# Wide attention with another order of its small steps, the first split of maxima ahead of two loads, and the last stores no longer waited for in their own stage

## The chip, the cores and the metric

The kernel runs on one core of one Trainium2 chip. Its five engines each follow their own list of instructions: TensorE (PE, with PEld for its weight loads), VectorE (DVE), ScalarE (ACT), GpSimd (POOL) and SyncE (SP), which here only issues transfers. They meet at semaphores. The metric is the device time of one execution in microseconds (us). Shorter is better.

## The reference

The model adds four blocks to `x` (8 batches, 512 rows, 256 columns); the context `ctx` has 1601 rows a batch.

```
x = x + tanh(g_xattn[0]) * attention_16_heads(layernorm(x), ctx, ctx)      # L0, bias bo on its output
x = x + tanh(g_ffn[0])   * one_of_4_experts(layernorm(x))
x = x + tanh(g_xattn[1]) * attention_1_head(layernorm(x), ctx, ctx)        # L1, rank-16 terms in Q, K, V
x = x + tanh(g_ffn[1])   * product_key_memory(batchnorm over rows, x)      # top 8 of 64 x 64 keys, 8 heads
```

In the wide (one-head) attention the products of weights are folded beforehand, so that per batch it is: `g = A xn^T`, scores `s = ctx g` (1601 x 512), softmax over the 1601 keys, `u = ctx^T p`, output `u^T C` divided by the sum of the probabilities and added to `x`.

## The kernel before

Five stages follow each other: `project`, `attend_heads`, `experts`, `attend_wide`, `memory`. Each is one block of code per engine. At the end of a block the engines meet before the next block starts. There is no scheduler: each engine does what the code lists, in that order, and an instruction that waits holds up all behind it.

**Wide attention (`attend_wide`).** One iteration `b` of 8 has these steps.

- PE: 13 score tiles of 128 keys (L1354, two matmuls each, which the trace shows as four rows), with small jobs hung behind certain tiles: the output product of batch `b-2` (`out_product`, L1394) behind tile `OUT_AT`, the transposes of the next normalised rows (L1322) behind `NORMS_AT`, the product with A (L1340) behind `MIX_AT`, the transposes of the finished rows of batch `b-3` (L1330) behind `LAST_AT`. Then `u` of batch `b-1`, two passes of 13 tiles (L1387). Within the first pass it transposes the running maxima (`turn_top`, L1365) and spreads them over the keys (`spread_rows`, L1372); within the second it sums the probabilities (`sums`, L1379). Score tile `kt` waits until ACT has emptied the buffer of tile `kt-4`.
- ACT: copies each score tile to `aw_sT` (L1492), then 13 exponentials (L1502), then a square root for the norm of batch `b+2` (L1464), one for the norm of the finished batch `b-2`, and then the copy of `u` to `aw_uT` (L1468, called by `copy`), for which `out_product` waits.
- DVE: running maxima (L1565), peaks (L1570, L1571), 13 subtractions `shift` (L1577), `invert` (the factor of one over the sum, L1583 and L1584), then `norms(b+2)` (L1525 and the lines of the helper `norm_tiles`: L91, L95, L97, L99, L101) and `last_norms(b-2)` with the same helper. A square root on ACT waits for L97 of its norm.
- POOL: gathers rows, then adds the 13 tiles of probabilities to `aw_total` (L1638). The first addition of batch `b` waits for `sums(b-1)`, which reads the same buffer.
- SP: stores the finished rows and their transposes (`last_out`, L1295, L1298), and at the stage's end waits for all these stores (L1314).

**Start of `attend_heads`.** SP loads the operands of four groups of heads, about 2.5 MB each (L422, L424, L431, L433, L457), the bias `bo` (L478), and with `rows_out` (L464) the three bfloat16 parts of the maxima of group 0. The first scores of unit 0 (L576) wait for these three, and those of unit 1 for its own three. The parts come from POOL's `split` (L773 to L776). POOL's list there is `spread`, `spread`, `split(0)`, `add_bias`, `split(1)`; `add_bias` (L789, L793) waits for `bo`.

**Start of `memory`.** POOL loads the transposed rows of tile 0 (L1769) and normalises them (L1778) for the first scores of PE (L1803); SP loads the two key tables of 4 MB (L1734) after the first two row tiles have landed. PE's first L1830 waits for the second table.

Of the kernel before, what the change touches and what calls it, by code (L numbers as in the profile page):

```python
# [22 lines left out]
P = 128  # L23
B, S, D = 8, 512, 256
KEYS = 1601
KC = D // P
# [5 lines left out]
G = H // HG  # L32
# [27 lines left out]
def gate(eng, sem):  # L60


    eng.sem_inc(sem, 1)
# [282 lines left out]
def attend_heads(nc, sem, t):  # L346
# [38 lines left out]
    with Stage(nc, "at") as st:  # L385
# [57 lines left out]
        with nc.Block() as block:  # L443
            @block.sync
            def _(sp):
# [30 lines left out]
                for g in range(G - 1):  # L476
                    load(0, g, False)
                sp.dma_start(bo[:, :], t["bo_in"]).then_inc(bo_in, 16)  # L478
                rows_out(0, 0)
# [746 lines left out]
def attend_wide(nc, sem, t):  # L1226
# [9 lines left out]
    NORMS_AT, OUT_AT, MIX_AT, LAST_AT = 4, 1, 7, 9  # L1236
    ROWS_AT, TOTAL_AT = (4, 9), 6
# [5 lines left out]
    with Stage(nc, "aw") as st:  # L1243
# [19 lines left out]
        l_turned, l_out, l_counted, l_stored = (sem(f"aw_last_{n}") for n in ("turned", "out", "counted", "stored"))  # L1263
# [5 lines left out]
        def turned_max(b):  # L1269

            return 2 + 3 * (b - 1) + 1 if b else 1
# [5 lines left out]
        def sums_mm(b):  # L1277

            return 2 + 3 * (b + 1) if b < B - 1 else 2 + 3 * (B - 1) + 1
# [3 lines left out]
        with nc.Block() as block:  # L1283
            @block.sync
            def _(sp):
# [28 lines left out]
                sp.wait_ge(l_stored, 16 * (1 + KC) * B + 1)  # L1314

            @block.tensor
            def _(pe):
# [57 lines left out]
                def sums(b):  # L1375

                    pe.wait_ge(summed, (b + 1) * (KT - 1))
                    for q in range(QT):
                        ins = nc.tensor.matmul(ps_p[:, 1, 0, q:q + 1], total[:, q * P:q * P + P], ones[:, 0:1], start=True, stop=True)  # L1379
                    ins.then_inc(peaks_mm, 1)  # L1380
# [26 lines left out]
                for b in range(B):  # L1407
# [18 lines left out]
                    for kt in range(KT):  # L1426
                        u_tile(b - 1, 0, kt)
                        if kt == ROWS_AT[0]:
                            turn_top(b)
                        elif kt == ROWS_AT[1]:  # L1430
                            spread_rows(b)
                    for kt in range(KT):
                        ins = u_tile(b - 1, 1, kt)
                        if kt == TOTAL_AT:
                            sums(b - 1)
# [24 lines left out]
            def _(act):  # L1460
# [22 lines left out]
                for b in range(B):  # L1483
# [19 lines left out]
                    if b + 2 < B:  # L1503
                        root(nth["next", b + 2])
                    if b >= 2:
                        root(nth["last", b - 2])
                    if b:
                        copy(uT[:, :, :], u_at[b - 1], u_mm, b, uT_out)
# [9 lines left out]
            def _(dve):  # L1518
# [72 lines left out]
                for b in range(B):  # L1591
# [4 lines left out]
                    if b >= 3:  # L1596
                        last_stats(b - 3)
                    find_peaks(b)
# [3 lines left out]
                    if b:  # L1602
                        invert(b - 1)
# [52 lines left out]
def memory(nc, sem, t, out):  # L1656
# [18 lines left out]
    with Stage(nc, "mt") as st:  # L1675
# [5 lines left out]
        xl, xb = st.sb("xl", [P, 2, KC, P]), st.sb("xb", [P, 2, KC, P])  # L1681
# [18 lines left out]
        mk, scale, offset = t["mk"], st.sb("scale", [P, KC]), st.sb("offset", [P, KC])  # L1700
        gamma, beta = t["gamma"], t["beta"]
        bmv, bve, bsd = st.sb("bmv", [P, KC, 2]), st.sb("bve", [P, KC]), st.sb("bsd", [P, KC])
# [23 lines left out]
        with nc.Block() as block:  # L1726
            @block.sync
            def _(sp):
                sp.dma_start(iota_f, t["m_iota_in"]).then_inc(iota_in, 16)
# [31 lines left out]
            def _(pool):  # L1761
                def token_rows(i, off):

                    n, s = 2 * i + off, off % 2
                    if off > 1:

                        pool.wait_ge(d_mm, (n - 1) * ND)
                        gate(pool, t["pool_gate"])
                    pool.dma_start(xl[:, s, :, :], t["xT_dram"][n]).then_inc(xl_in[s], 16)  # L1769
# [115 lines left out]
            def _(act):  # L1885
# [35 lines left out]
                def first():  # L1921
                    act.wait_ge(b_var, 1)
                    nc.scalar.activation(bsd[:, :], bve[:, :], ACT.Sqrt).then_inc(b_sd, 1)
                    for c in range(2):
                        scores_out(0, 0, c)
# [172 lines left out]
def build(nc, ins, out, debug=None):  # L2098

    with ExitStack() as ctx:  # L2100
        def sem(name):
# [36 lines left out]
            "gates_opened": sem("gates_opened"), "release_x": x_life.close, "bstats": bstats,  # L2138
# [103 lines left out]
```

## Time and profile before

| | us |
|---|---|
| median of 3 runs (3486.71 to 3490.65) | 3489.04 |
| the profiled execution, whole | 3490.57 |
| its span in the trace | 3488.9 |
| project (PE's last wait before heads ends) | 0 to 231.6 |
| heads, first scores of unit 0 | from 293.66 |
| wide attention, first transposes to last statistics | 1784.1 to 2295.3 |
| memory | 2298.8 to the end |

Over the span PE is busy 95%, DVE 72%, ACT 46% and POOL 13%. In a row of the timeline the first number is the start, the second the stretch that the merged instructions cover, and the brackets at its end hold the idle time just before it on that engine and who ended it. All times are us from the start of the span. A "releaser" is who signalled last.

### The profile page before, as it was taken

Reading aid. Unit: us, or ns where it says so; the run is one execution under the profiler, and the core shown is the slowest. Engines: PE = TensorE matmul, PEld = TensorE weight load, DVE = VectorE, ACT = ScalarE, POOL = GpSimd, SP = SyncE. Lnnn points to the kernel's source line nnn. Section 1 sums busy time; section 2 is a strip of 40 time slices with the busy share of each in tenths; the row PEclk is TensorE's granted clock in tenths of the full one; section 3 lists DMA queues with packets and bytes.
Section 4 is the critical chain, followed back from the end, with each engine's and each line's share of the span. In section 5 each row is a group of like instructions: output and inputs, shape, how many; then the busy total and the mean of one; then the engine's idle time right before and its main releaser. Section 6 shows DMA issues by size and latency. Waiting matters only on the chain. (4 is left out here: it accounts for less than half of the span.)

```text
span 3488.9 us, 61035 instructions
## 1 busy us (share of the span) xinstructions
PE 3307.3 (95%) x21500; PEld 1962.3 (56%) x21500; DVE 2506.5 (72%) x5513; ACT 1602.7 (46%) x2882; POOL 452.8 (13%) x538
## 2 busy tenths in 40 slices
PE   9988999999999999779979989969999999999999
PEld 5652222222222222568844444538889888898988
DVE  5557898889898986520035565568888888888885
ACT  5535888888888888212223323312222222222221
POOL 0022111111111100110014241300000000000000
PEclk9987999999999999879989999979999999999999
DMA  7687676757575650421111221130000000000000
GB/s 275 247 232 96 99 105 100 105 100 105 100 106 99 94 72 15 171 92 49 38 63 50 75 81 62 43 129 10 11 12 11 12 9 11 12 11 12 9 12 8
DMA packets 148231, 256.70 MB, mean 74 GB/s; under 512 B 23848, under 2 KB 99472, under 8 KB 147536
## 3 DMA queue, kind: packets, MB, share of 16 engines
q1 hardware_dynamic: 132752, 218.29, 29.4%
q0 software_dynamic: 10288, 31.21, 2.7%
q10 hardware_dynamic: 5008, 5.00, 0.5%
q8 instruction: 86, 1.41, 0.2%
q14 instruction: 97, 0.79, 0.1%
HBM read 170.38 MB, written 83.64 MB: 73 GB/s over the span
## 5 line engine op out<-in xcount | busy, mean ns | idle before, releaser
L724 DVE TENSOR_REDUCE at_pmax<-at_psm 128x2 f32<-128x1024 f32 (+1 forms) x832 | 945.0, 1179 | 127.7 <-PE at_psm L552 123.0
L661 ACT ACTIVATE ring<-at_pss 128x512 f32<-128x512 f32 (+1 forms) x1664 | 895.1, 595 | 194.0 <-PE at_pss L576 190.9
L576 PE MATMUL at_pss<-at_qs,at_ks 99*128 99x512 bf16 (+1 forms) x1664 | 512.0, 386 | 14.7 <-ACT ring L661 7.2
L1830 PE MATMUL mt_psd<-mt_xl,mt_key_in 128*128 128x128 f32 x4096 | 491.8, 279 | 0.2 <-DMA mt_key_out<-m_out 0.2
L1830 PEld LDWEIGHTS mt_psd<-mt_xl,mt_key_in 128*128 128x128 f32 x4096 | 470.3, 193 | 1.6 <-DMA mt_key_out<-m_out 0.3
L1856 PE MATMUL mt_psu<-mt_key_out,mt_g 128*128 128x256 f32 x2048 | 447.4, 379 | 1.3 <-DVE mt_g L2066 1.3
L584 PE MATMUL at_pso<-ring,at_vw 128*32 128x512 f32 (+1 forms) x3328 | 444.0, 605 | 0.0
L1856 PEld LDWEIGHTS mt_psu<-mt_key_out,mt_g 128*128 128x128 f32 x2048 | 386.7, 190 | 52.6 <-DVE mt_g L2066 1.4
L576 PEld LDWEIGHTS at_pss<-at_qs,at_ks 99*128 99x128 bf16 (+1 forms) x1664 | 116.5, 98 | 489.7 <-ACT ring L661 428.0
L1918 ACT ACTIVATE mt_g<-mt_psd 128x512 f32<-128x512 f32 x256 | 152.9, 598 | 349.7 <-PE mt_psd L1830 349.4
L550 PE MATMUL at_psm<-at_ks,at_qs 64*128 64x512 bf16 (+1 forms) x1024 | 272.1, 344 | 10.2 <-DVE at_pmax L724 8.9
L552 PE MATMUL at_psm<-at_kh,at_qh 64*128 64x512 bf16 (+1 forms) x1024 | 272.4, 344 | 0.0
L550 PEld LDWEIGHTS at_psm<-at_ks,at_qs 64*128 64x128 bf16 x1024 | 78.5, 94 | 228.6 <-issue 152.0
L2066 DVE TENSOR_TENSOR mt_g<-mt_psc,mt_g 128x512 f32<-128x512 f32 x256 | 164.0, 683 | 56.8 <-PE mt_psc L1845 56.2
L1894 ACT ACTIVATE mt_sims<-mt_psx 128x512 f32<-128x512 f32 x64 | 38.3, 598 | 349.8 <-PE mt_psx L1803 349.8
L1354 PE MATMUL aw_pss<-aw_gT,wide_ctxT 128*128 128x512 f32 (+1 forms) x416 | 186.9, 599 | 5.0 <-DVE aw_sT L1577 2.8
L1845 PEld LDWEIGHTS mt_psc<-mt_hot_w,mt_hot_m 128*128 128x128 f16 x4096 | 136.8, 98 | 36.2 <-issue 34.8
L1196 ACT ACTIVATE ex_hid<-ex_psh,ex_b 128x256 f32<-128x256 f32 x136 | 62.5, 474 | 205.9 <-PE ex_psh L1161 205.8
L1565 DVE TENSOR_TENSOR aw_top<-aw_top,aw_sT 128x512 f32<-128x512 f32 (+1 forms) x88 | 64.5, 732 | 127.7 <-ACT aw_sT L1492 127.1
L584 PEld LDWEIGHTS at_pso<-ring,at_vw 128*32 128x32 f32 (+1 forms) x3328 | 65.8, 108 | 152.4 <-ACT ring L661 130.1
L2036 DVE TENSOR_TENSOR mt_hot_m<-mt_iota_m,mt_picksT 128x2048 f16<-128x2048 f16 x128 | 150.2, 1213 | 0.0
L1769 POOL DMA_DIRECT2D mt_xl<-xT_dram x32 | 18.6, 580 | 1012.4 <-PE mt_psd L1830 976.7
(232 smaller groups left out, 4193.1 us busy)
## 6 DMA issues: line engine op xcount, KB each, us to landing
at_ks<-k_dram SPq DMA_DIRECT2D x192, 200.1 KB, 6.4
k_dram<-pj_kp SPq DMA_DIRECT2D x24, 800.5 KB, 5.4
xs_dram<-at_qf POOLq DMA_DIRECT2D x68, 256.0 KB, 3.1
v_dram<-pj_v SPq DMA_DIRECT2D x8, 1664.0 KB, 6.6
at_vd<-v_dram SPq DMA_DIRECT2D x32, 416.0 KB, 10.1
wide_ctxT<-ctxT SPq DMA_DIRECT2D x8, 1601.0 KB, 7.2
at_kh<-k_dram SPq DMA_DIRECT2D x124, 100.1 KB, 5.4
at_qs<-q_dram SPq DMA_DIRECT2D x192, 64.0 KB, 6.8
```

Of the source, the lines that this page charges most:

```text
L550: nc.tensor.matmul(ps_m[:, n % MBANKS, 0, to:to + w], qs[0:MAX_ROWS, g, 2 * p, q * P:q * P + P], ks[0:MAX_ROWS, g, 2 * p, a:a + w], start= ...
L552: ins = nc.tensor.matmul(ps_m[:, n % MBANKS, 1, to:to + w], qh[MAX_ROWS:2 * MAX_ROWS, g, p, q * P:q * P + P], kh[MAX_ROWS:2 * MAX_ROWS, g, ...
L576: nc.tensor.matmul(ps_s[0:r, score_slot(u, n), :], ks[:, g, j, kt * P:kt * P + r], qs[:, g, j, :], start=True, stop=True).then_inc(s_mm, 1)
L584: nc.tensor.matmul(ps_o[j * 32:(j + 1) * 32, :], vw[0:r, g % 2, kt * HG + j, :], pr[0:r, (NST * g + n) % PRING, :], start=kt == 0, stop=kt ...
L661: nc.scalar.activation(pr[0:r, (NST * g + n) % PRING, :], ps_s[0:r, score_slot(u, n), :], ACT.Exp, scale=SCALE).then_inc(expd, 1)
L724: nc.vector.tensor_reduce(heads, found, AX.X, ALU.max).then_inc(m_red, 1)
L1354: ins = nc.tensor.matmul(ps_s[0:r, slot(b, kt), :], ctxT[:, b % 2, k, kt * P:kt * P + r], gT[:, b % 2, k, :], start=k == 0, stop=k == KC - 1)
L1830: ins = nc.tensor.matmul(ps_d[:, j % 2, y * P:y * P + P], key_in[:, k, j * YB + y, :], xl[:, s, k, :], start=k == 0, stop=k == KC - 1)
L1856: ins = nc.tensor.matmul(ps_u[:, 0:D], g[:, off % 2, y, :], key_out[:, y, :], start=y == 0, stop=y == YH - 1)
L1918: nc.scalar.activation(g[:, off % 2, j * YB:(j + 1) * YB, :], ps_d[:, j % 2, :].rearrange("p (y n) -> p y n", n=P), ACT.Gelu).then_inc(g_o ...
L2036: return nc.vector.tensor_tensor(dst.rearrange("p n (m r) -> p n m r", r=RUN), iota[:, 0:cols].rearrange("p (m r) -> p m r", r=RUN).unsque ...
L2066: nc.vector.tensor_tensor(gv, ps_c[:, tb % CRING, h, :].rearrange("p (n u y) -> p y u n", u=2, y=YH), gv, ALU.mult).then_inc(w_out, 1)
```

## The change

In `attend_heads` SP issues the maxima of group 0 behind two loads of groups instead of three; the third load and the bias come behind them. In `attend_wide` the small jobs of PE move to later tiles, `sums(b-1)` moves from the second pass of `u` to the first, ahead of `turn_top`, ACT copies `aw_uT` ahead of the second square root, and DVE calls `invert` ahead of `find_peaks`. SP no longer waits for the last stores at the end of the stage; instead those in `memory` who read the stored rows, or whose buffers may lie where the stored rows lay, wait for the same semaphore, and POOL's first two loads only for the stores of the first batch. `sums` gets two waits more, for ACT's copies of transposes out of the bank that it writes.

```diff
@@ attend_heads, SP
-                for g in range(G - 1):
+                for g in range(2):
                     load(0, g, False)
+                rows_out(0, 0)
+                load(0, 2, False)
                 sp.dma_start(bo[:, :], t["bo_in"]).then_inc(bo_in, 16)
-                rows_out(0, 0)
                 load(0, G - 1, False)
                 rows_out(0, 1)
@@ attend_wide
-    NORMS_AT, OUT_AT, MIX_AT, LAST_AT = 4, 1, 7, 9
-    ROWS_AT, TOTAL_AT = (4, 9), 6
+    NORMS_AT, OUT_AT, MIX_AT, LAST_AT = 6, 2, 9, 11
+    ROWS_AT = (4, 9)
...
-                sp.wait_ge(l_stored, 16 * (1 + KC) * B + 1)
@@ PE
                 def sums(b):
                     pe.wait_ge(summed, (b + 1) * (KT - 1))
+                    pe.wait_ge(xnT_out, min(b + 3, B))
+                    if b >= 2:
+                        pe.wait_ge(l_out, b - 1)
...
                         if kt == ROWS_AT[0]:
+                            sums(b - 1)
                             turn_top(b)
...
                         ins = u_tile(b - 1, 1, kt)
-                        if kt == TOTAL_AT:
-                            sums(b - 1)
@@ ACT
                         root(nth["next", b + 2])
+                    if b:
+                        copy(uT[:, :, :], u_at[b - 1], u_mm, b, uT_out)
                     if b >= 2:
                         root(nth["last", b - 2])
-                    if b:
-                        copy(uT[:, :, :], u_at[b - 1], u_mm, b, uT_out)
@@ DVE
+                    if b:
+                        invert(b - 1)
                     find_peaks(b)
                     dve.wait_ge(peaks_mm, max_rows(b))
                     for kt in range(KT):
                         shift(b, kt)
-                    if b:
-                        invert(b - 1)
@@ memory, SP
+                sp.wait_ge(t["wide_stored"], PER_BATCH * B + 1)
                 sp.dma_start(iota_f, t["m_iota_in"]).then_inc(iota_in, 16)
@@ memory, POOL
+                    pool.wait_ge(t["wide_stored"], PER_BATCH * (B if off > 1 else 1) + 1)
                     pool.dma_start(xl[:, s, :, :], t["xT_dram"][n]).then_inc(xl_in[s], 16)
@@ memory, ACT, behind the square root
+                    act.wait_ge(t["wide_stored"], PER_BATCH * B + 1)
```

ACT, wide attention, from the exponentials of one batch to the score tiles of the next; `aw_sd` is a square root, `aw_uT` the copy of `u`. Before:

```order
L1502 ACTIVATE aw_sT<-aw_sT 65x512
L1464 ACT_TABLE_LOAD
L1464 ACTIVATE aw_sd<-aw_ve 128x4 x2
L1468 ACTIVATE aw_uT<-aw_psw 128x1024
L1492 ACTIVATE aw_sT<-aw_pss 128x512 x6
```

And now:

```order
L1505 ACTIVATE aw_sT<-aw_sT 65x512
L1467 ACT_TABLE_LOAD
L1467 ACTIVATE aw_sd<-aw_ve 128x4
L1471 ACTIVATE aw_uT<-aw_psw 128x1024
L1467 ACTIVATE aw_sd<-aw_ve 128x4
L1495 ACTIVATE aw_sT<-aw_pss 128x512 x8
```

The copy of `u` stands between the two roots; the score tiles still stand behind both.

PE, wide attention, from the first pass of `u` to the next batch's norms; `aw_psp<-aw_ones,aw_total` are the sums, `cmat` marks the output product. Before:

```order
L1387 MATMUL aw_psw<-aw_sT,aw_ctx 128x512 x5
L1365 MATMUL aw_psp<-ident_sb,aw_top 128x128 x4
L1387 MATMUL aw_psw<-aw_sT,aw_ctx 128x512 x5
L1372 MATMUL aw_pss<-aw_rows,aw_ones 128x512
L1387 MATMUL aw_psw<-aw_sT,aw_ctx 128x512 x10
L1379 MATMUL aw_psp<-aw_ones,aw_total 128x1 x4
L1387 MATMUL aw_psw<-aw_sT,aw_ctx 128x512 x6
L1354 MATMUL aw_pss<-aw_gT,wide_ctxT 128x512 x4
L1394 MATMUL aw_psw<-cmat,aw_uT 128x256 x8
L1354 MATMUL aw_pss<-aw_gT,wide_ctxT 128x512 x6
L1322 MATMUL aw_psp<-ident_sb,aw_xn 128x128 x8
```

And now:

```order
L1391 MATMUL aw_psw<-aw_sT,aw_ctx 128x512 x5
L1383 MATMUL aw_psp<-aw_ones,aw_total 128x1 x4
L1366 MATMUL aw_psp<-ident_sb,aw_top 128x128 x4
L1391 MATMUL aw_psw<-aw_sT,aw_ctx 128x512 x5
L1373 MATMUL aw_pss<-aw_rows,aw_ones 128x512
L1391 MATMUL aw_psw<-aw_sT,aw_ctx 128x512 x16
L1355 MATMUL aw_pss<-aw_gT,wide_ctxT 128x512 x6
L1398 MATMUL aw_psw<-cmat,aw_uT 128x256 x8
L1355 MATMUL aw_pss<-aw_gT,wide_ctxT 128x512 x8
L1323 MATMUL aw_psp<-ident_sb,aw_xn 128x128 x8
```

The sums stand 16 matmuls of `u` earlier, the output product one tile later, the transposes two tiles later. The matmuls are the same.

SP, start of `attend_heads`, from the end of the third group's load (before) and of the second's (now) on; `at_mpart` are the parts of the maxima. Before:

```order
L457 DMA at_vd<-v_dram 128x832
L478 DMA at_bo<-bo 128x256
L464 DMA at_qs<-at_mpart 1x16x128 x3
L422 DMA at_ks<-k_dram 16x4x1601
L424 DMA at_qs<-q_dram 16x4x512
```

And now:

```order
L457 DMA at_vd<-v_dram 128x832
L464 DMA at_qs<-at_mpart 1x16x128 x3
L422 DMA at_ks<-k_dram 16x4x1601
...
L457 DMA at_vd<-v_dram 128x832
L480 DMA at_bo<-bo 128x256
L422 DMA at_ks<-k_dram 16x4x1601
```

The parts stand ahead of the third group's 21 transfers, and the bias with these behind the parts.

## Rows read from the trace of the kernel before

**Rows 1.** Windows (start:end, length, busy time of each engine, clock, DMA), wide attention.
```profile
1888.10:1942.70 54.60, 54.60 (x151) 26.59 (x150) 31.11 (x49) 21.08 (x32) 21.09 (x17) 1.00 0.21 70
...
2082.00:2086.00 4.00, 4.00 (x11) 3.14 (x10) 3.10 (x4) 0.00 (x0) 3.40 (x4) 0.50 0.05 11
```

**Rows 2.** Waits of PE, 1820 to 2300: in total, times, longest.
```profile
PE aw_psw L1394 <- ACT aw_uT L1468: 25.5, 5, 6.3
```

**Rows 3.** Timeline of PE, wide attention, batches 3, 5 and 7.
```profile
1942.74 3.60 PE L1354 MATMUL aw_pss<-aw_gT,wide_ctxT 128*128 128x512 f32 x8
...
2071.16 3.60 PE L1354 MATMUL aw_pss<-aw_gT,wide_ctxT 128*128 128x512 f32 x8
2081.03 6.34 PE L1394 MATMUL aw_psw<-cmat,aw_uT 128*128 128x256 f32 x16 [6.28 <-ACT aw_uT L1468]
...
2092.36 1.04 PE L1322 MATMUL aw_psp<-ident_sb,aw_xn 128*128 128x128 f32 x8
...
2200.53 3.60 PE L1354 MATMUL aw_pss<-aw_gT,wide_ctxT 128*128 128x512 f32 x8
```

**Rows 4.** Timeline of ACT, turn from batch 4 to 5.
```profile
2071.41 0.20 ACT L1464 ACTIVATE aw_sd<-aw_ve 128x4 f32<-128x4 f32 x1 [4.86 <-DVE aw_ve L97]
2079.86 0.20 ACT L1464 ACTIVATE aw_sd<-aw_ve 128x4 f32<-128x4 f32 x1 [8.24 <-DVE aw_ve L97]
2079.97 1.01 ACT L1468 ACTIVATE aw_uT<-aw_psw 128x1024 f32<-128x1024 f32 x1
```

**Rows 5.** Timeline of DVE, turn from batch 4 to 5.
```profile
2056.72 7.86 DVE L1577 TENSOR_TENSOR aw_sT<-aw_sT,aw_pss 128x512 f32<-128x512 f32 x13 [3.73 <-PE aw_pss L1372]
...
2067.54 1.28 DVE L1525 SCALAR_TENSOR_TENSOR x_rows<-aw_y,opened_sb,x_rows 128x1024 f32<-128x1024 f32 x1
...
2079.01 0.82 DVE L97 TENSOR_SCALAR aw_ve<-aw_mv 128x4 f32<-128x4 f32 x1
```

**Rows 6.** Timeline of POOL, turn from batch 4 to 5.
```profile
2066.21 1.27 POOL L1638 TENSOR_TENSOR aw_total<-aw_sT 128x512 f32<-128x512 f32 x1 [41.72 <-PE aw_psp L1379]
```

**Rows 7.** Timelines of DVE and POOL, batch 0.
```profile
1826.43 7.86 DVE L1577 TENSOR_TENSOR aw_sT<-aw_sT,aw_pss 128x512 f32<-128x512 f32 x13 [1.22 <-PE aw_pss L1372]
1834.21 1.27 DVE L1525 SCALAR_TENSOR_TENSOR x_rows<-aw_y,opened_sb,x_rows 128x1024 f32<-128x1024 f32 x1
...
1828.46 1.27 POOL L1638 TENSOR_TENSOR aw_total<-aw_sT 128x512 f32<-128x512 f32 x1 [35.82 <-ACT aw_sT L1502]
```

**Rows 8.** Timeline of PE, scores of batch 1.
```profile
1843.86 1.85 PE L1322 MATMUL aw_psp<-ident_sb,aw_xn 128*128 128x128 f32 x8 [3.05 <-DVE aw_xn L101]
1845.50 6.28 PE L1354 MATMUL aw_pss<-aw_gT,wide_ctxT 128*128 128x512 f32 x12
```

**Rows 9.** SP's wait and a row of the chain, turn to memory.
```profile
SPq L1283 <- DMA xT_dram<-keys: 2.5, 1, 2.5
...
2299.28 2.52 DMA mt_xl<-xT_dram
```

**Rows 10.** Timeline, start of heads; last row: issue to landing of the maxima's transfers.
```profile
271.86 0.88 POOL L762 COPY at_vw<-at_vd 128x832 f32<-128x832 f32 x1 [14.26 <-DMA at_vd<-v_dram]
...
283.28 1.89 SPq L464 DMA_DIRECT2D at_qs<-at_mpart  x3
...
292.35 0.93 POOL L789 TENSOR_SCALAR at_bo<-at_bo,opened_sb 128x256 f32<-128x256 f32 x1 [9.10 <-DMA at_bo<-bo]
293.37 18.55 POOL L793 TENSOR_TENSOR x_rows<-x_rows,at_bo 128x1024 f32<-128x1024 f32 x8
293.66 1.44 PE L576 MATMUL at_pss<-at_qs,at_ks 99*128 99x512 bf16 x3 [6.74 <-DMA at_qs<-at_mpart]
...
323.69 0.28 POOL L773 CAST at_mpart<-at_mfull 16x128 bf16<-16x128 f32 x1 [11.78 <-ACT at_mfull L677]
...
330.36 0.60 PE L576 MATMUL at_pss<-at_qs,at_ks 99*128 99x512 bf16 x2
...
DMA to landing us min/median/max: 1.7/2.3/8.8
```

More of the change, by code:

```diff
@@ L1262, in attend_wide @@
         u_mm, uT_out, o_mm, o_out = (sem(f"aw_{n}") for n in ("u_mm", "uT_out", "o_mm", "o_out"))
-        l_turned, l_out, l_counted, l_stored = (sem(f"aw_last_{n}") for n in ("turned", "out", "counted", "stored"))
+        l_turned, l_out, l_counted = (sem(f"aw_last_{n}") for n in ("turned", "out", "counted"))
+        l_stored = t["wide_stored"]
         def slot(b, kt):
@@ L1269, in turned_max @@
         def turned_max(b):
-            return 2 + 3 * (b - 1) + 1 if b else 1
+            return 2 + 3 * (b - 1) + 2 if b else 1
         def max_rows(b):
@@ L1277, in sums_mm @@
         def sums_mm(b):
-            return 2 + 3 * (b + 1) if b < B - 1 else 2 + 3 * (B - 1) + 1
+            return 2 + 3 * b + 1
         u_at = [ps_w[:, :, :]] * (B - 1) + [ps_s[:, 0:KC, :]]
@@ L1680, in memory @@
         gate_down = st.sb("gate_down", [P, 1])
-        xl, xb = st.sb("xl", [P, 2, KC, P]), st.sb("xb", [P, 2, KC, P])
         xr = st.sb("xr", [P, 2, D])
@@ L1700, in memory @@
         mk, scale, offset = t["mk"], st.sb("scale", [P, KC]), st.sb("offset", [P, KC])
+        PER_BATCH = 16 * (1 + KC)
         gamma, beta = t["gamma"], t["beta"]
+        xl, xb = st.sb("xl", [P, 2, KC, P]), st.sb("xb", [P, 2, KC, P])
         bmv, bve, bsd = st.sb("bmv", [P, KC, 2]), st.sb("bve", [P, KC]), st.sb("bsd", [P, KC])
@@ L2137, in build @@
             "ident": ident, "ident_in": ins["ident"], "gates": gates, "gates_in": ins["gates"], "opened": opened,
-            "gates_opened": sem("gates_opened"), "release_x": x_life.close, "bstats": bstats,
+            "gates_opened": sem("gates_opened"), "wide_stored": sem("aw_last_stored"), "release_x": x_life.close, "bstats": bstats,
             "x_dram": nc.dram_tensor("x_dram", (NT, P, D), F32, kind="Internal").ap(),
```

## The prediction

> **What bounds the kernel now.** I read the busy shares first: PE is busy for 95% of the span, so a change that adds no matmul can only win where PE stands idle or runs at the lower clock. The list of PE's waits in wide attention names the place: it waited 25.5 us for the copy `aw_uT`, in 5 waits of which the longest is 6.3 [rows 2]. The timeline shows one [rows 3]: after two score tiles of batch 5 (2071.16 to 2074.75) PE idles 6.28 us and takes the output product at 2081.03. That row covers 6.34 us, and the window from 2082 to 2086 shows why it is long: the granted clock is 0.50, which is 1.2 instead of 2.4 GHz [rows 1]. ACT's rows name the cause [rows 4]: the copy runs at 2079.97, right behind a second square root at 2079.86 that had waited 8.24 us for DVE, while `u` had been ready since about 2071.2. A neighbour gives the size of a batch without the wait: from 1888.10 to 1942.70 (batch 2) PE is busy 54.60 of 54.60 us at clock 1.00 [rows 1]. Batches 3 to 6 take (2200.53 - 1942.74) / 4 = 64.45 us each [rows 3].
>
> **Wide attention, batches 3 to 6.** These batches hold the work of batch 2 and one group of eight transposes more, at most 1.04 us [rows 3], so 55.64 us with no wait. The stake is 64.45 - 55.64 = 8.81 us a batch: 6.28 of idle time, the rest lower clock. It is won if `aw_uT` is there when PE wants it, and if nothing else is late. I follow the turn from batch 4 to 5.
>
> PE now does the sums (some 0.8 us) ahead of the transposes of the maxima, so the spread of the maxima and DVE's subtractions move from 2056.72 to 2057.5 [rows 5]. They take 7.86 and end at 2065.4. POOL's first addition waited until 2066.21 for the sums [rows 6]; now only the exponentials hold it. Batch 0 is the pattern, since it has no sums ahead of it [rows 7]: the additions start 2.03 us after the subtractions, here at 2059.6, and beside them the 13 subtractions still take 7.86. `invert` no longer stands behind the subtractions. There it cost DVE the way from 2064.6 to 2067.54 [rows 5], so the norm starts at 2065.4 instead of 2067.54, and the first root, 3.9 us behind that start [rows 4, 5], comes at 2069.3 instead of 2071.41. The next instruction on ACT is now the copy, which waits only for the end of `u`. PE's work up to there is the same, so the copy runs at about 2071.4 to 2072.4. PE wants it after three tiles, at 2071.16 + 3 x 1.72 = 2076.3. Cover: 3.9 us.
>
> What is late next is the second root: the first score tile's copy stands behind it on ACT, and PE's fifth tile waits for that. DVE reached the second L97 at 2079.01, 11.47 us behind the start of the norm [rows 5]; from 2065.4 that is 2076.9, with its 0.82 us 2077.7, and the root and the first copy end by 2078.6. PE reaches its fifth tile at 2076.3 + 3.4 (output product) + 1.7 (fourth tile) = 2081.5. Cover: 2.9 us. So I take the whole stake, 4 x 8.81 = 35.2 us. The bounds are nothing lost, 35.2, and a new stall of the old kind in each batch, which keeps nothing.
>
> A rule of the Trainium skill bears on that cover. First the row: the fused addition at 1834.21 began straight behind the subtractions and took 1.27 with POOL adding beside it [rows 7], no longer than the 1.28 at 2067.54 [rows 5]. In "SBUF — State Buffer", section "Who interferes with whom", the skill says that a DVE instruction with both inputs in SBUF contends with a GpSimd instruction that reads SBUF, and that the one that comes second is blocked for the whole of the other. By that rule the fused addition would have to wait for one addition of 1.27 now that POOL runs from 2059.6; by the row it waits for none. With the wait the cover shrinks from 2.9 to 1.6 us and the sum stays; two such waits and a little more would open the first rival below, and I put 3 of its hundredths there.
>
> **Batch 1.** PE waited 3.05 us for DVE's `aw_xn` before the transposes, which then took 1.85 instead of 1.04, and twelve rows took 6.28 where eight take 3.60, so twelve about 5.3 [rows 3, 8]. The transposes now stand two tiles later, and two tiles are 3.4 us, more than the wait. Gain 3.05 + 0.81 + 0.95 = 4.8 us. Bounds: 3.05 if the clock stays low as long, 4.8 if not. I take 4.8, since the work that fills the gap is matmul work. Batches 2 and 7 had no such wait and keep their time. The later places of the other jobs cost nothing: each keeps its distance to its reader, and the transposes of the finished rows are read by ACT 2.5 us before the sums want the bank.
>
> **Turn to memory.** SP waited 2.5 us for the last stores before the engines could meet [rows 9]. Without it POOL's load of tile 0 moves from 2299.28 up by 2.5. It took 2.52 us and now runs beside those stores, 768 KB. I take 2.2 us; bounds 1.5 and 2.5. DVE's statistics, the two key tables and all behind them move with it, since the tables wait for the two row tiles. ACT and SP wait for the last stores in the new place until about 2298.4, earlier than their next work is due, and POOL's two other waits are met.
>
> **Heads, start.** PE waited 6.74 us for the maxima's parts, to 293.66; they had been issued from 283.28 on but took up to 8.8 instead of the median 2.3 us, behind the load of group 2 [rows 10]. Now only loads 0 and 1 stand ahead, and these had landed at 271.86. The third part is issued at about 284.6 and lands at 286.9, so unit 0 starts at 287.0, 6.7 us earlier. But the bias lands behind load 2, which starts only at 285.2. From 271.86 to 292.35 that pair took 20.5 us when it queued behind others; fresh, I take 19.8, so it lands at 305.0. The bounds are 299.8 (at the 14.6 us in which the next load of the same size passed, until the DMA engines went quiet at 306.9) and 305.7. Then POOL's bias takes 19.6 us (292.35 to 311.92 [rows 10]) to 324.6, and `split(1)` stands behind it on POOL. Before, it began at 323.69 after an idle of 11.78; now it would be wanted at 317.0 and begins at 324.6. From its start to the landing of the last part are 1.7 (281.62 to 283.28 for unit 0) + 1.3 (to the issue of the third) + 2.3 = 5.3 us, so unit 1 can start at 329.9. It started at 330.36 [rows 10] and PE would now be there at 323.7: a stall of 6.2 us, of the size that in wide attention brought the clock to 0.50. There it cost 8.81 - 6.28 = 2.5 us; PE is the busiest engine here too, but its matmuls are less dense: 2.0. So heads give 0.5 and take 2.0: 1.5 us slower. Bounds: 6.7 faster (bias early enough) and 2.5 slower.
>
> **Sum.** -35.2 - 4.8 - 2.2 + 1.5 = -40.7 us. The profiled execution took 3490.57 us, so 3449.9; it stands 1.5 above the median of the runs, from which the same sum gives 3448.3. I predict 3448.5.
>
> **The rivals.**
> - *The second root takes the copy's place.* PE stops at the fifth tile instead. For it: the cover of 2.9 us rests on DVE beside POOL, where a scalar operation takes up to 1.3 us instead of 0.35. Against: even a root as late as the old one (2079.86) lets the fifth tile go by 2080.9. If it stops PE by 2 us with 2 of low clock behind, 4 batches lose 16: 3465.
> - *The whole gain of heads stays.* The bias lands by about 299, so `split(1)` is in time: 8 us less, 3441. For it: the next load passed in 14.6 us. Against: it had been queued while another ran.
> - *Slower.* POOL's additions now lie beside the 13 subtractions in every batch. If each had to wait for an addition, 1.3 us instead of 0.6, they would take 17 and end 9.3 us later; `aw_uT` would come at 2079.9, a stall of 3.6 + 2 in the tails of batches 1 to 6, and 5.5 before `u` of batch 7. The fifth tile would wait 2 more in four of them. That is 6 x 5.6 + 5.5 + 8 = 47 against 40.0 gained: less the 0.7 that the other parts give, 3497, and it decides from 1.13 us a subtraction on. Against it: 7.86 us for 13 beside POOL in batch 0 [rows 7].
> - *The change doesn't do what it says*, with the wait kept by a condition that I have not seen: 3489.
>
> **Chances.** Forecast 0.76, second root 0.09, heads keep their gain 0.11, slower 0.02, no change 0.02. The forecast's own range is 3444 to 3454; with its neighbours, 3438 to 3459. A measurement of this kernel tells a difference from about 0.2%, 7 us: faster 0.96, same 0.02, slower 0.02.
>
> **What would show it.** PE's list of waits keeps no entry of several us for `aw_uT`; batches 3 to 6 take 55.6 us each at clock 1.00; POOL's additions start at most 2.5 us behind DVE's subtractions; the fifth score tile follows the fourth without a gap. PE's wait before the transposes in batch 1 is gone. POOL's first load in memory starts about 2.5 us closer to the last store's issue. In heads, unit 0 starts near 287.0 and unit 1 near 329.9, with a wait for `at_mpart` of about 6 us and a clock under 1 behind it, and POOL's bias from about 305. A gap at the fifth tile, or subtractions over 0.7 us each, would prove me wrong.

## The result

| kernel | us, median (lowest to highest) | runs |
|---|---|---|
| before | 3487.88 (3486.0 to 3490.65) | 4 |
| after | 3451.2 (3447.5 to 3452.92) | 4 |

The ratio is 0.9893, 95% interval 0.9878 to 0.9907: the change is 36.7 us, about 1.1%, faster. The profiled execution of the kernel after took 3450.29 us with a span of 3448.6, so the two traces lie 40.3 us apart. The forecast sum of 40.7 was made from the first trace, so it is set against 40.3 below; against the medians it is 4.0 us too large. Timed again later on one chip, the same two kernels lay 30.6 us apart (section "Heads"). Line numbers of the kernel after are one to six higher in the places shown here.

### The profile page after: what moved, and what is told of

The parts are those of the page before. It is cut to its first block and busy times, and to the rows that moved or that the text cites. A ratio compares the mean times of both kernels' runs of the same rounds, so it can differ in the third digit from the quotient of the medians.

```text
span 3448.6 us, 61045 instructions
## 1 busy us (share of the span) xinstructions
PE 3297.8 (96%) x21500; PEld 1953.3 (57%) x21500; DVE 2483.1 (72%) x5513; ACT 1602.0 (46%) x2882; POOL 452.9 (13%) x538
## 5 line engine op out<-in xcount | busy, mean ns | idle before, releaser
L1219 DVE COPY ex_xsT<-ex_pst 128x512 f32<-128x512 f32 x17 | 11.8, 692 | 188.8 <-PE ex_psh L1162 188.8
## 6 DMA issues: line engine op xcount, KB each, us to landing
at_vd<-v_dram SPq DMA_DIRECT2D x32, 416.0 KB, 10.5
```

## The profile after

Windows over batches 3 to 6 of wide attention (start:end, length, busy time of PE, PEld, DVE, ACT and POOL, granted clock, DMA share, GB/s), first of before, then of after:

```profile
1942.74:2200.53 257.79, 232.70 (x634) 116.28 (x632) 149.07 (x258) 88.14 (x137) 76.24 (x62) 0.95 0.21 67
```

```profile
1941.50:2163.17 221.67, 221.67 (x634) 109.87 (x633) 131.70 (x253) 86.39 (x134) 78.50 (x62) 1.00 0.25 78
```

PE was idle for 25.1 of 257.8 us and at a mean clock of 0.95; now it is busy in all of its 221.7 us at 1.00. A batch takes 55.42 us instead of 64.45. The list of PE's waits (1820 to 2260) keeps one short entry for the copy where [rows 2] had 25.5 us:

```profile
PE aw_psw L1398 <- ACT aw_uT L1471: 0.4, 1, 0.4
```

The timeline of PE behind the turn from batch 4 to 5 answers to [rows 3]:

```profile
2052.33 5.31 PE L1355 MATMUL aw_pss<-aw_gT,wide_ctxT 128*128 128x512 f32 x12
2057.48 3.62 PE L1398 MATMUL aw_psw<-cmat,aw_uT 128*128 128x256 f32 x16
2060.94 7.03 PE L1355 MATMUL aw_pss<-aw_gT,wide_ctxT 128*128 128x512 f32 x16
```

None of the three rows has brackets: no idle time before the output product, none before the fifth tile (2060.94 is the fourth; the fifth follows within the row). ACT, DVE and POOL at the same place answer to [rows 4], [rows 5] and [rows 6]:

```profile
2050.45 0.20 ACT L1467 ACTIVATE aw_sd<-aw_ve 128x4 f32<-128x4 f32 x1 [1.83 <-DVE aw_ve L97]
2052.53 1.02 ACT L1471 ACTIVATE aw_uT<-aw_psw 128x1024 f32<-128x1024 f32 x1 [1.88 <-PE aw_psw L1391]
2058.89 0.20 ACT L1467 ACTIVATE aw_sd<-aw_ve 128x4 f32<-128x4 f32 x1 [5.34 <-DVE aw_ve L97]
2059.01 1.55 ACT L1495 ACTIVATE aw_sT<-aw_pss 128x512 f32<-128x512 f32 x3
```

```profile
2038.79 7.86 DVE L1580 TENSOR_TENSOR aw_sT<-aw_sT,aw_pss 128x512 f32<-128x512 f32 x13 [3.67 <-PE aw_pss L1373]
2046.57 1.28 DVE L1528 SCALAR_TENSOR_TENSOR x_rows<-aw_y,opened_sb,x_rows 128x1024 f32<-128x1024 f32 x1
```

```profile
2040.82 1.27 POOL L1641 TENSOR_TENSOR aw_total<-aw_sT 128x512 f32<-128x512 f32 x1 [32.05 <-ACT aw_sT L1505]
```

Take 18.83 us (2071.16 - 2052.33) off the times of the forecast and they can be read against these rows: subtractions 2038.7 (measured 2038.79), POOL 2040.8 (2040.82), first root 2050.5 (2050.45), copy 2052.6 (2052.53), PE wants it at 2057.5 (2057.48). The copy is done at 2053.55, 3.9 us early. The last score copy of the three at 2059.01 ends at 2060.56, and PE's fifth tile comes at about 2062.7.

The fused addition starts straight behind the subtractions with POOL adding beside it. The contention is there all the same, on POOL's side: the one of its additions that runs beside it took 2.48 us instead of 1.27.

```profile
2046.50 2.48 POOL L1641 TENSOR_TENSOR aw_total<-aw_total,aw_sT 128x512 f32<-128x512 f32 x1
```

It is so at each of the six places in this trace and the six in the trace of before (2.33 to 2.48 us); [rows 7] shows only the first addition, not the one beside the fused addition, which took 2.46. This agrees with the Trainium skill ("SBUF — State Buffer", section "Who interferes with whom"), by which a DVE instruction with two inputs in SBUF contends with a GpSimd instruction that reads SBUF. DVE pays elsewhere: four normalising operations take 5.28 us beside POOL's additions and 1.38 without them, and the step ahead of a root 0.82 instead of 0.34.

```profile
2050.90 5.28 DVE L101 TENSOR_SCALAR aw_xn<-x_rows,aw_mv,aw_rstd 128x256 f32<-128x256 f32 x4
2059.35 1.38 DVE L101 TENSOR_SCALAR aw_xl<-x_rows,aw_mv,aw_rstd 128x256 f32<-128x256 f32 x4
```

So, by the same difference, about 3.9 of the 8.24 us for which the second root waited in [rows 4] were DVE beside POOL. Taking the additions out of its way was not tried.

Batch 1 answers to [rows 8]: the eight transposes have lost their wait and their low clock, but two others stay.

```profile
1830.03 5.31 PE L1355 MATMUL aw_pss<-aw_gT,wide_ctxT 128*128 128x512 f32 x12
1838.15 3.53 PE L1355 MATMUL aw_pss<-aw_gT,wide_ctxT 128*128 128x512 f32 x4 [2.80 <-DVE aw_sT L1580]
1842.62 5.42 PE L1355 MATMUL aw_pss<-aw_gT,wide_ctxT 128*128 128x512 f32 x12 [0.94 <-ACT aw_sT L1495]
1847.88 1.04 PE L1323 MATMUL aw_psp<-ident_sb,aw_xn 128*128 128x128 f32 x8
```

From the first scores of batch 1 to the first product with the exponentials it is 32.46 us (1830.03 to 1862.49), before 37.40: 4.9 less. At the turn to memory SP, POOL and PE answer to [rows 9]:

```profile
2256.49 1.60 SPq L1300 DMA_DIRECT2D xT_dram<-keys  x2
2258.98 0.58 POOL L1775 DMA_DIRECT2D mt_xl<-xT_dram  x1 [39.43 <-DMA x_dram<-x_rows]
2262.58 3.78 PE L1809 MATMUL mt_psx<-mk,mt_xb 128*128 128x512 f32 x4 [7.67 <-POOL mt_xb L1784]
```

The list of SP's waits shows the old wait in its new place, behind the meeting of the engines, where it delays only a table:

```profile
SPq L1734 <- DMA xT_dram<-keys: 2.2, 1, 2.2
```

From the last transposes (2252.97) to PE's first product of memory it is 9.6 us instead of 12.2. And heads, the timeline of POOL, SP and PE, against [rows 10]:

```profile
280.24 0.28 POOL L774 CAST at_mpart<-at_mfull 16x128 bf16<-16x128 f32 x1 [9.43 <-ACT at_mfull L678]
281.89 1.90 SPq L464 DMA_DIRECT2D at_qs<-at_mpart  x3
285.48 1.46 PE L577 MATMUL at_pss<-at_qs,at_ks 99*128 99x512 bf16 x3
305.30 0.93 POOL L790 TENSOR_SCALAR at_bo<-at_bo,opened_sb 128x256 f32<-128x256 f32 x1 [23.43 <-DMA at_bo<-bo]
325.08 0.28 POOL L774 CAST at_mpart<-at_mfull 16x128 bf16<-16x128 f32 x1 [0.19 <-POOL x_rows L794]
329.76 1.01 PE L577 MATMUL at_pss<-at_qs,at_ks 99*128 99x512 bf16 x2 [6.59 <-issue]
```

```profile
320.00:325.00 5.00, 3.17 (x24) 0.66 (x16) 3.45 (x3) 2.65 (x6) 4.88 (x3) 1.00 0.62 106
325.00:330.00 5.00, 0.24 (x1) 0.14 (x2) 0.00 (x0) 0.00 (x0) 1.85 (x5) 0.58 0.01 2
330.00:335.00 5.00, 5.00 (x18) 0.60 (x16) 2.36 (x2) 2.46 (x5) 0.06 (x1) 0.50 0.00 0
335.00:340.00 5.00, 5.00 (x20) 0.71 (x20) 2.36 (x2) 2.56 (x6) 0.81 (x1) 0.56 0.90 130
```

Unit 0 no longer waits, the bias lands at 305.2, `split(1)` follows POOL's additions 0.19 us behind their end, and PE stands 6.59 us before unit 1. That row names no releaser ("issue"); that it is the parts is read from the times, since the third part lands at 329.67 and unit 1 starts at 329.76. Then it works at 0.50 (1.2 GHz) for nearly 10 us. `split(2)` (362.17) comes 32.4 us behind unit 1's first scores; in the kernel before it came 28.1 us behind them (358.48 - 330.36), at full clock. That is 4.3 us more for the same work at the lower clock, and 3.5 us lost by the start of wide attention (first transposes 1787.65 instead of 1784.14).

By stages, from the two timelines: up to wide attention +3.5, wide attention -41.3 (batch 1 -4.9, batches 3 to 6 -36.1, the rest -0.3), turn to memory -2.6, memory 0.0. Together -40.4 us.

## One part at a time

Four kernels ran once each, with a profile. The yardsticks are read from the timelines: the time of a batch from the scores of batch 3 to those of batch 7, over four; and batch 1 from its first scores to its first product with the exponentials.

**The copy ahead of the second root, alone, in the kernel before.**

```
                     if b + 2 < B:
                         root(nth["next", b + 2])
+                    if b:
+                        copy(uT[:, :, :], u_at[b - 1], u_mm, b, uT_out)
                     if b >= 2:
                         root(nth["last", b - 2])
-                    if b:
-                        copy(uT[:, :, :], u_at[b - 1], u_mm, b, uT_out)
```

> The kernel before with one edit: ACT copies `aw_uT` ahead of the second root. My theory: the queue order on ACT was the whole cause of the 6.28 us, so this edit alone wins batches 3 to 6. At the turn from batch 4 to 5 the copy follows the first root, at about 2071.6, and PE wants it at 2074.75: no wait there, 55.6 us a batch instead of 64.45. The second root then waits until about 2079.8 for DVE, as before, and the first score copy ends at about 2080.7, while PE reaches its fifth tile at about 2081.5: still hidden, by 0.8 us. Time about 35 below the kernel before, some 3453 to 3456. Batch 1 keeps its wait of 3.05 us for `aw_xn`. The rival: the denominators had to be moved too, because the late second root now stops PE's fifth score tile in each batch, by 2 us and more with low clock behind it: 59 us a batch, some 3470.

Measured: 3441.72 us, beside 3483.81 of the kernel before on that chip. A batch takes 55.47 us. The timeline of ACT at the turn from batch 4 to 5, and below it that of PE:

```profile
2043.44 0.20 ACT L1464 ACTIVATE aw_sd<-aw_ve 128x4 f32<-128x4 f32 x1 [4.87 <-DVE aw_ve L97]
2043.55 1.01 ACT L1468 ACTIVATE aw_uT<-aw_psw 128x1024 f32<-128x1024 f32 x1
2051.91 0.21 ACT L1464 ACTIVATE aw_sd<-aw_ve 128x4 f32<-128x4 f32 x1 [7.36 <-DVE aw_ve L97]
2052.03 2.27 ACT L1492 ACTIVATE aw_sT<-aw_pss 128x512 f32<-128x512 f32 x4
```

```profile
2043.18 3.60 PE L1354 MATMUL aw_pss<-aw_gT,wide_ctxT 128*128 128x512 f32 x8
2046.62 3.62 PE L1394 MATMUL aw_psw<-cmat,aw_uT 128*128 128x256 f32 x16
2050.07 5.31 PE L1354 MATMUL aw_pss<-aw_gT,wide_ctxT 128*128 128x512 f32 x12
```

The copy no longer waits, and PE takes the output product straight behind its second tile. The second root is as late as before (8.7 us behind the batch's start, in [rows 3, 4] it was 8.70 too), and it stops nobody: the fifth tile, inside the row of 2050.07, has no gap. The theory holds in its mechanism and in its 35 us (35.9 in batches 3 to 6); the rival falls. Exchanging two calls gives by itself nearly all of the 36.1 us that the whole change gained there. (The single time is 11 us under the expectation; the section on heads tells why.)

**The denominators ahead of the maxima, alone.**

```
                         if kt == ROWS_AT[0]:
+                            sums(b - 1)
                             turn_top(b)
...
                         ins = u_tile(b - 1, 1, kt)
-                        if kt == TOTAL_AT:
-                            sums(b - 1)
@@ DVE
+                    if b:
+                        invert(b - 1)
                     find_peaks(b)
...
-                    if b:
-                        invert(b - 1)
```

(with the counts and the three waits of `sums` as in the kernel after)

> The kernel before with one edit: PE's sums and DVE's reciprocals of the denominators go ahead of the maxima, the copy stays behind both roots. My theory: this only moves DVE's norms, and so the second root, up by about 2.1 us; PE's wait for `aw_uT` shrinks from 6.28 to about 4.2 us and stays in all of batches 3 to 6, about 62.3 us each: 8 to 9 us below the kernel before. The rival: the denominators were the cause; then the wait falls under 1 us and the time goes down by 30 or more.

Measured: 3471.6 us. 61.35 us a batch; the wait is the one expected:

```profile
2065.74 4.64 PE L1397 MATMUL aw_psw<-cmat,aw_uT 128*128 128x256 f32 x13 [4.14 <-ACT aw_uT L1470]
```

The wait shrank by 2.14 and stayed. The gain in batches 3 to 6 is 12.4 us, not 8 to 9, since the shorter wait also costs less clock (table below). The rival falls.

**The places of the other jobs, alone.**

```
-    NORMS_AT, OUT_AT, MIX_AT, LAST_AT = 4, 1, 7, 9
+    NORMS_AT, OUT_AT, MIX_AT, LAST_AT = 6, 2, 9, 11
```

> The kernel before with one edit: the places of PE's other jobs between the score tiles (4, 1, 7, 9 become 6, 2, 9, 11). My theory: in batch 1 the wait for `aw_xn` goes and with it 4.9 us; in batches 3 to 6 PE does one tile more before it wants `aw_uT`, so its wait is 4.6 instead of 6.28 us, 62.7 us a batch, 7 us over the four. Together 12 below the kernel before. The rival: the places matter only in batch 1 and the wait in batches 3 to 6 has another releaser, so it stays at 6.3 and the gain is 5.

Measured: 3470.03 us. 62.21 us a batch with waits of 4.56 us:

```profile
2066.03 4.33 PE L1394 MATMUL aw_psw<-cmat,aw_uT 128*128 128x256 f32 x11 [4.56 <-ACT aw_uT L1468]
```

In batches 3 to 6 the wait is the 4.6 us expected, and the gain 9.0 us instead of 7. Batch 1 takes 34.19 us here, not 32.46. The same code of this stretch comes in two forms, which go with the moment at which PE's clock goes down in it:

| batch 1, us | old places | new places |
|---|---|---|
| clock down later (PE's first wait 2.80 us) | 37.40 (before) | 32.45 to 32.46 (after and three more) |
| clock down earlier (first wait 1.5 to 1.7) | 35.76 to 35.78 (four traces) | 34.19 (five traces) |

Here is PE in the second form, with the old places and the copy alone, where [rows 8] had a wait of 3.05:

```profile
1817.37 6.46 PE L1354 MATMUL aw_pss<-aw_gT,wide_ctxT 128*128 128x512 f32 x12
...
1835.04 1.09 PE L1322 MATMUL aw_psp<-ident_sb,aw_xn 128*128 128x128 f32 x8 [1.42 <-DVE aw_xn L101]
```

So the expected 4.9 us are there in the first form only; in the second the places are worth 1.6. Both first traces happened to show the first form. Over all traces the means are 36.1 and 33.4 us: 2.7. What decides between the forms was not tried.

**The copy's place taken back in the kernel after** (the first diff, the other way round).

> The kernel after with one edit taken back: ACT copies `aw_uT` behind the second root again. My theory: the copy comes at about 6.7 us behind the batch's first score tile, ends at 7.7, and PE wants it at 5.15: a wait of 2.6 us in each of batches 3 to 6, and by the clock up to 2.5 more, so 58.0 to 60.5 us a batch instead of 55.42, 10 to 20 us above the kernel after. The rival, that the copy's place adds nothing once the denominators and the jobs stand where they do now: no wait, 55.4 us a batch. The old kernel's whole loss back (36 us) would say that the copy's place is all there is.

Measured: 3460.34 us. 58.53 us a batch (the last three 58.10), with waits of 2.4:

```profile
2067.60 3.72 PE L1398 MATMUL aw_psw<-cmat,aw_uT 128*128 128x256 f32 x16 [2.42 <-ACT aw_uT L1471]
```

12.4 us come back in batches 3 to 6, within the expectation. So in batches 3 to 6 the copy alone is worth 36, the two other edits of wide attention together 23.7 (36.1 - 12.4), and everything 36.1: the parts overlap, since they shorten the same wait.

These kernels measure what a wait costs beyond itself in this stage, against 55.42 us a batch at full clock:

| wait of PE, us | batch, us | lost beyond the wait |
|---|---|---|
| 2.42 (last three batches) | 58.10 | 0.3 |
| 2.43 (batch 3 of the same trace) | 59.80 | 2.0 |
| 4.14 | 61.35 | 1.8 |
| 4.56 | 62.21 | 2.2 |
| 6.28 | 64.45 | 2.8 |

The first two rows are the same wait without and with a fall of the clock behind it (mean granted clock 0.97 over batch 3, 1.00 over each of the other three), so the wait's length alone does not set the price. The last three rows are means over four batches.

**The turn to memory** was not run by itself. From the last transposes to memory's first product with the key table it took 37.48, 37.16, 37.08, 37.35, 37.13 and 37.15 us in the six traces without this part and 34.56 to 35.00 in the eight with it: 2.5 us on the means, whatever else was changed.

## Heads

**The edit of heads, alone in the kernel before, and taken back in the kernel after.**

```
-                for g in range(G - 1):
+                for g in range(2):
                     load(0, g, False)
+                rows_out(0, 0)
+                load(0, 2, False)
                 sp.dma_start(bo[:, :], t["bo_in"]).then_inc(bo_in, 16)
-                rows_out(0, 0)
                 load(0, G - 1, False)
```

> The kernel before with the edit of heads alone (maxima's parts of unit 0 ahead of load 2, the bias behind it). My theory: unit 0 starts about 7 us earlier, the bias lands at about 305, POOL is free at about 325, unit 1 starts within 1 us of its old 330.4 but behind a stall of 6 to 7 us, and the clock stays at 0.50 for about 9 us after it: 3 to 4 us slower than before at the start of unit 2 and at the end of heads. The term on record for this was 1.5 slower (0.5 gained, 2.0 lost to the clock). The rival: the 3.3 us that heads lost in the kernel after has nothing to do with this edit (it ran 1.4 us ahead already before unit 0), then heads end within 1 us of the kernel before.

Measured: 3492.27 us, beside 3489.27 of the kernel before.

```profile
306.07 0.93 POOL L790 TENSOR_SCALAR at_bo<-at_bo,opened_sb 128x256 f32<-128x256 f32 x1 [24.12 <-DMA at_bo<-bo]
...
330.53 1.01 PE L577 MATMUL at_pss<-at_qs,at_ks 99*128 99x512 bf16 x2 [8.40 <-issue]
```

`split(2)` is at 363.07, 4.6 us later than in the trace of before. Against the trace of before the theory holds, and the wait of 8.40 us belongs to this edit; how much of the loss is the draw of that one trace comes out below.

> The kernel after with the edit of heads taken back. My theory: unit 0 at about 293, unit 1 at about 330, no stall before unit 1, clock 1.00 there; the span is 3 to 4 us shorter than that of the kernel after, about 3447 for the time. By the term on record it would be 1.5 shorter. The rival: wide and memory gained something that this gives back, so that the span doesn't move.

Measured: 3450.95 us, beside 3450.29 of the kernel after. Not 3 to 4 us less, nothing. The theory seemed to fall, until the timeline of PE showed a longer wait than the 6.74 us of before:

```profile
296.80 1.44 PE L576 MATMUL at_pss<-at_qs,at_ks 99*128 99x512 bf16 x3 [10.72 <-DMA at_qs<-at_mpart]
```

The wait for the parts was 6.74 us in [rows 10], 10.72 here; with the copy alone and with the places alone, which have the same order of heads, there was none. In this order the parts queue behind load 2, and the DMA engines, always full then, do not move it at the same rate in each execution. The window from 272 to 283 us, first of the copy alone, then of the kernel with its heads undone:

```profile
272.00:283.00 11.00, 9.13 (x49) 5.45 (x48) 8.25 (x9) 1.46 (x3) 1.40 (x4) 0.50 1.08 137
```

```profile
272.00:283.00 11.00, 9.11 (x49) 5.43 (x48) 8.26 (x9) 1.46 (x3) 2.27 (x5) 0.50 1.09 118
```

| trace with the old order of heads | GB/s, 272 to 283 | wait of unit 0, us | `split(3)` at |
|---|---|---|---|
| places alone | 152 | 0 | 386.60 |
| copy alone | 137 | 0 | 385.80 |
| denominators alone | 133 | 3.53 | 389.57 |
| heads undone, second time | 126 | 5.71 | 391.56 |
| copy alone, second time | 126 | 5.65 | 392.10 |
| before | 125 | 6.74 | 393.24 |
| heads undone | 118 | 10.72 | 397.10 |

The new order gave 396.60, 396.95, 397.83 and 398.84. It takes the luck out, but at the dear end: on the mean 6.7 us later than the 390.9 of the old order. What the old order loses, it loses while the clock is at 0.50 anyway (in all seven traces from 280 to 290 us); the new one waits where it had been 1.00. What makes the rate differ was not tried. It may in part be the chip: 152, 137 and 133 GB/s come from one chip, 126 twice from another, 118 from a third (that of the trace of before is not on record). But the wait differs on one chip too, 0 to 3.53 us on the first.

**The bias ahead of unit 0's parts.** The stretch from 272 to 283 us is all but free of transfers in the kernel after (DMA share 0.01), and `bo` is one transfer that nothing needs to precede.

```
                 for g in range(2):
                     load(0, g, False)
+                sp.dma_start(bo[:, :], t["bo_in"]).then_inc(bo_in, 16)
                 rows_out(0, 0)
                 load(0, 2, False)
-                sp.dma_start(bo[:, :], t["bo_in"]).then_inc(bo_in, 16)
                 load(0, G - 1, False)
                 rows_out(0, 1)
```

> The kernel after, with the load of the bias `bo` issued ahead of unit 0's maxima's parts, straight behind loads 0 and 1 (the parts still go ahead of load 2). My theory: what cost heads their gain was only the bias behind load 2. Now it lands before 280, POOL adds it from about 282 to 302, `split(1)` starts when ACT has its maxima, at about 316, and PE finds unit 1's parts at or shortly behind 322.6. The only thing left in their way is load 3, which ends at about 321 to 323: a wait of 0 to 2 us. Units 1 to 7 then run about 10 us ahead of the kernel after: 3440, 3442 if the wait is 2. The rival: unit 1 waits for its parts behind load 3, as unit 0 did behind load 2 in the kernel before (8.8 us instead of 2.3), so it starts at about 328 with low clock behind it: 3448.

Measured: 3437.17 us.

```profile
281.65 0.92 POOL L790 TENSOR_SCALAR at_bo<-at_bo,opened_sb 128x256 f32<-128x256 f32 x1
...
323.42 0.59 PE L577 MATMUL at_pss<-at_qs,at_ks 99*128 99x512 bf16 x2 [1.67 <-issue]
```

The bias starts at once, `split(1)` at 315.00 and PE waits 1.67 us for parts behind the end of load 3. As expected, in this one trace.

**Unit 1's parts ahead of load 3 as well** (`rows_out(0, 1)` above `load(0, G - 1, False)`).

> As the version with the bias first, and unit 1's maxima's parts issued ahead of load 3 as well. My theory: the parts land about 2.3 us behind their issue at about 319, so unit 1 starts without a wait at about 322.6; load 3 is issued at about 320, lands by about 342 and is wanted by PE's maxima of unit 3, from about 356 on. 3439 to 3440, the same as or up to 2 us better than with the bias alone. The rival: load 3, now later, pushes the loads of the next batch behind it, and a unit further on waits: over 3442.

Measured: 3445.64 us; the rival holds. Unit 1 starts without a wait, but load 3 and the load behind it now run together to beyond 350, unit 2's parts, issued at 352.83, come late, and the clock falls there:

```profile
361.61 0.59 PE L577 MATMUL at_pss<-at_qs,at_ks 99*128 99x512 bf16 x2 [3.72 <-issue]
```

**Four kernels timed together**, five rounds on one chip, where the kernel before took 3485.4 (3477.59 to 3490.37, 7 runs). Draws of 0 to 10.7 us in heads would make such a spread of 13 us in the same program; these seven runs have no trace that shows it.

> The kernel after once more, timed beside the next three. In every look at its order of heads so far unit 1 waited 6.6 to 8.4 us for its parts, so its times should lie close together, within about 5 us, around 3451. It is the yardstick: the part of heads costs it what the next two give back.

> The kernel after with the bias load issued ahead of unit 0's parts. In the look neither unit 0 nor unit 1 waited over 2 us. My theory: this order depends on no race between a load and the parts, so the gain is there in every run: 11 to 14 us below the kernel after, about 3438, with a spread under 4 us. The rival: the look was a lucky one, and in some runs load 3 delays the parts of unit 1; then the spread is 8 us or more and the median gain under 8.

> The kernel after with the old order in heads (parts of unit 0 behind load 2). My theory, new since the looks: in this order unit 0's wait is a matter of luck, 0 to 10.7 us in the six traces that have it, so the times spread over some 10 us, between about 3440 and 3451, with a median some 3 to 7 us below the kernel after. The rival is the claim made from the first pair of traces alone: a fixed 3.3 us between them, and a spread of 3 us.

> The kernel before with the copy of `aw_uT` ahead of the second root and nothing else. My theory: it lacks the gain of the places (4 to 5 us in the wide stage) and that of the turn to memory (2.4) and has the old luck of heads: about 6 us above the kernel after with its heads undone, so level with the kernel after within 4 us, 3446 to 3452, spread 10. The rival, from the single look (3441.7): it beats the kernel after by 8 us or more, because the rest of the change is worth nothing.

| kernel | median | lowest to highest, 4 runs each | ratio to before, 95% |
|---|---|---|---|
| after | 3454.79 | 3451.91 to 3455.3 | 0.9911 (0.9891 to 0.993) |
| after, bias first | 3445.28 | 3437.29 to 3446.2 | 0.9879 (0.9856 to 0.9902) |
| after, heads undone | 3444.29 | 3439.15 to 3445.18 | 0.9878 (0.9857 to 0.9899) |
| before, copy alone | 3448.19 | 3444.49 to 3450.42 | 0.9892 (0.9872 to 0.9913) |

The kernel after is steady, as expected. With its heads undone it is 10.5 us faster, more than the 3 to 7 that I had expected from single traces, with a spread of 6 instead of 10; the rival (3.3 us, fixed) falls. The copy alone lies 6.6 us below the kernel after where I expected them level within 4, and 3.9 above the kernel with heads undone, which the turn (2.5) and batch 1 (1.6) make up. The bias first is not free of luck, although I had claimed it: three of its four runs lie 7 to 9 us above the fourth. The profiled one is of the slower kind:

```profile
325.61 0.59 PE L577 MATMUL at_pss<-at_qs,at_ks 99*128 99x512 bf16 x2 [3.73 <-issue]
```

```profile
325.00:330.00 5.00, 4.39 (x18) 0.74 (x18) 2.36 (x2) 2.63 (x5) 0.23 (x1) 0.69 0.00 0
330.00:335.00 5.00, 5.00 (x21) 0.70 (x20) 2.45 (x3) 2.79 (x7) 0.64 (x1) 0.63 0.93 139
```

Two more us of wait behind load 3 than in the first trace of this kernel, and then the low clock that the first didn't have: `split(2)` comes 31.2 us behind the start of unit 1 instead of 28.1. So here the rival is right on the spread (8.9 us), and the gain over the kernel after is 9.5, under the 11 to 14 that I expected. The best that was measured is therefore either of these two, level with each other and about 10 us, or 0.3%, below the kernel after; each of their runs lies below each of its. With the order of heads left as it was, the change would have gained about 10 us more.

## Why the prediction was right, and where it was not

- **Batches 3 to 6**, forecast 35.2 us: 36.1 between the traces. Mechanism, times and covers (3.9 us for the copy; the fifth tile without a gap) came as said. The batch is 55.42 instead of 55.64 us because the eight transposes took 0.9 and not 1.04 us of PE's way. The copy alone shows that a second root as late as the old one stops nobody, so the case in which it takes the copy's place needed a root later still.
- **POOL beside DVE**: 13 subtractions still take 7.86 us, so the slower case did not come. The fused addition did not wait either, but the reading of [rows 7], that nothing waits there, was half of it: POOL's addition beside it took 2.46 us instead of 1.27. A scalar operation of DVE beside POOL took up to 1.19 us (L1584 in the trace of before), not the 1.3 of the first rival.
- **Batch 1**, forecast 4.8: 4.9 between the two traces, but I took one trace's wait of 3.05 us as the kernel's. Four of five traces with the old places had 1.4 to 1.6 us there, and then the step is worth 1.6 instead of 4.9.
- **Turn to memory**, forecast 2.2 (1.5 to 2.5): 2.6 between the traces, 2.5 on the means.
- **Heads**, forecast 1.5 slower: 3.5 slower between the traces, and 10.5 us between the kernel after and the same kernel with this edit undone, on medians timed together. The chain came as said: unit 0 at 285.48 (forecast 287.0, the stage ran 1.4 ahead there), bias at 305.3 (305.0), `split(1)` at 325.08 (324.6), unit 1 at 329.76 (329.9), a wait of 6.6 (6.2). The mis-sized term is the clock behind it: the 2.0 taken because the matmuls are "less dense" measured 4.3, since the clock stayed at 0.50 for nearly 10 us. And the base was a draw: in [rows 10] unit 0 had waited 6.74 us, where the same order waits 0 to 10.7.

The sum came out at -40.4 against -40.7 since the errors cancel: 0.9 + 0.1 + 0.4 us more gained, 2.0 more lost, and the rest of wide attention gave 0.3. The range held because it was wider than any of them, and by luck of the draws besides. Both traces had the first form of batch 1, and the trace of before had a wait of 6.74 us in heads where others with its order had none; with a draw of the cheap kind on that side the gain would have been some 7 us smaller. In the later timing it was 30.6 us (3485.4 to 3454.79), a quarter under the sum.

## What to carry over

When an engine stands before work whose input has long been ready, read what stands in the producer's queue ahead of it: one instruction that waits for a third engine was worth 36 us here, and moving it was worth more than the two edits that shortened the wait. A transfer that must be early should be issued when the DMA engines are empty, and the whole chain behind it followed: the parts went ahead of a load, and the bias that went behind that load then cost more than the parts had won. Where a wait stands behind a transfer or a clock change, a second trace of the same code comes before its price: two of the waits priced here were draws.

## What the runs showed of the chip

- The rate at which full DMA engines (share 1.08 to 1.10) moved the same load was 118 to 152 GB/s in seven traces on at least three chips, and the wait behind it 10.7 to 0 us.
- Beside DVE's fused addition with both inputs in SBUF, one POOL addition took 2.33 to 2.48 us instead of 1.27, twelve times in two traces, while DVE's 1.28 us did not change. Beside the same additions four DVE operations of 128x256 took 5.28 us instead of 1.38, and 13 subtractions with one input in PSUM the same 7.86.
- The same wait costs different amounts of clock: 2.4 us cost 0.3 or 2.0 us more in wide attention, 6.3 us cost 2.8 more there, and 6.6 us cost 4.3 more in heads. After a wait of 1.67 us in heads the next 5 us window had a granted clock of 1.00, after 3.73 us it had 0.69 and the one behind it 0.63.
- In batch 1 the same instructions took 37.40 or 35.77 us with the old places and 32.46 or 34.19 with the new ones, together with the moment at which PE's clock went down in them. The form that is dear with the old places is the cheap one with the new.
